# A fused attention and feed-forward kernel: four loads for the first group, two helpers moved, and a new order of calls

## What is computed

```python
x = x + attn_ref(layernorm(x), ...)   # linear attention, then a feed-forward of 1024 with gelu
x = x + ffn_ref(layernorm(x), ...)    # ternary weights, gelu, layernorm over 1024
```

## Time and profile before

| | |
|---|---|
| median of 3 runs | 464.06 us (463.73 to 464.63) |
| the profiled execution | 462.83 us |
| its span on the core, first to last instruction | 461.1 us |
| mean granted TensorE clock | 0.993 |
| PE (TensorE matmul) busy | 441.1 us, 96% |
| DVE (VectorE) busy | 369.7 us, 80% |
| ACT (ScalarE) busy | 321.1 us, 70% |
| POOL (GpSimd) busy | 185.7 us, 40% |
| chain that ended last | PE 84%, DVE 6%, issue 4%, POOL 2%, ACT 2%, DMA 1% |

### The profile page before, as it was taken

How to read it: one execution, slowest core, us unless ns; L and a number is a source line. 1 busy time by engine, 2 the same in 40 slices (tenths; PEclk the granted TensorE clock), 3 DMA queues, 4 the chain that set the end, 5 groups by cost and what they waited for, 6 DMA issues and landing times.

```text
span 461.1 us, 8907 instructions
## 1 busy us (share of the span) xinstructions
PE 441.1 (96%) x2980; PEld 399.3 (87%) x2980; DVE 369.7 (80%) x1212; ACT 321.1 (70%) x603; POOL 185.7 (40%) x188
## 2 busy tenths in 40 slices
...
GB/s 245 110 92 137 1 2 1 1 23 2 8 61 2 25 0 70 1 24 1 2 69 2 23 1 71 0 25 1 0 70 1 24 1 24 1 1 23 7 19 47
DMA packets 10045, 14.09 MB, mean 31 GB/s; under 512 B 784, under 2 KB 9104, under 8 KB 9488
## 3 DMA queue, kind: packets, MB, share of 16 engines
...
...
## 4 chain that ended last, share of the span: by engine, by line
PE 84%; DVE 6%; issue 4%; POOL 2%; ACT 2%; DMA 1%; DVEq 0%; POOLq 0%; ACTq 0%
PE bank_f L410 13%; PE bank_p L440 12%; PE bank_y L201 6%; PE bank_y L202 6%; PE bank_y L203 6%; PE bank_f L201 6%; PE bank_f L203 6%; PE bank_y L424 6%; PE bank_f L202 6%; PE bank_a L201 4%; PE bank_a L203 4%; PE bank_a L202 4%; PE bank_a L209 3%; PE bank_f L209 2%; PE bank_a L308 1%
## 5 line engine op out<-in xcount | busy, mean ns | idle before, releaser
L1146 POOL TENSOR_TENSOR rs<-ve,neg_half 128x2 f32<-128x2 f32 x48 | 33.7, 702 | 208.6 <-DVE ve L835 207.2
L896 DVE TENSOR_TENSOR h_lo<-bank_f,h_hi 128x512 fp32r<-128x512 f32 x60 | 41.3, 688 | 34.7 <-ACT h_hi L649 34.6
L201 PE MATMUL bank_y<-wf_hi,h_hi 128*128 128x256 f32 x240 | 67.1, 280 | 0.0
L202 PE MATMUL bank_y<-wf_lo,h_hi 128*128 128x256 f32 x240 | 67.0, 279 | 0.0
L203 PE MATMUL bank_y<-wf_hi,h_lo 128*128 128x256 f32 x240 | 67.0, 279 | 0.0
L440 PE MATMUL bank_p<-wpj_t,g_hi 128*128 128x256 f32 x256 | 64.3, 288 | 0.6 <-DVE y_yc L1040 0.6
L1031 DVE SCALAR_TENSOR_TENSOR g_lo<-bank_y,vec,g_hi 128x256 fp32r<-128x256 f32 x128 | 55.7, 477 | 9.3 <-ACT g_hi L678 8.2
L440 PE MATMUL bank_p<-wpj_t,g_lo 128*128 128x256 f32 x256 | 62.3, 279 | 0.0
L678 ACT ACTIVATE g_hi<-bank_y,vec 128x256 fp32r<-128x256 f32 x128 | 53.1, 481 | 10.3 <-PE bank_y L424 8.1
L641 ACT ACTIVATE bank_f<-bank_f,f_bias 128x512 f32<-128x512 f32 x64 | 42.4, 664 | 23.8 <-PE bank_f L203 23.4
L410 PE MATMUL bank_f<-wfc_t,z3T_hi 128*128 128x512 f32 x128 | 53.6, 419 | 0.5 <-DVE z3T_lo L896 0.5
...
## 6 DMA issues: line engine op xcount, KB each, us to landing
...
h<-in_f SPq DMA_DIRECT2D x1, 1024.0 KB, 7.6
y_yc<-in_f SPq DMA_DIRECT2D x1, 1024.0 KB, 10.0
h<-in_fc SPq DMA_DIRECT2D x1, 1024.0 KB, 4.8
h<-in_pj SPq DMA_DIRECT2D x1, 1024.0 KB, 4.7
...
```

The source lines that it names most:

```text
L201: pe.matmul(ps, w[0], r[0], start=start, stop=False, skip_group_check=skip)
L202: pe.matmul(ps, w[0], r[1], start=False, stop=False, skip_group_check=skip)
L896: dve.tensor_tensor(dst, b, hi.bitcast(F32), ALU.subtract).then_inc(s[ready], 1)
L1146: pool.tensor_tensor(rs[n][:, 2 * h:2 * h + 2], ve[n][:, 2 * h:2 * h + 2], neg_half[:, 0:2], ALU.pow).then_inc(s[f"ln{n + 1}_rs"], 1)
```

## The change

1. `load_x(0)` issues four loads, one tile of 128 tokens each, in place of two. The even tiles signal `x_first0` and `x_first1`, the odd tiles the old semaphores. VectorE takes the statistics of the even tiles in a new `ln1_st0`, and `ln1_stats(0, h)` makes only those of the odd tile and then goes on as before.
2. `wide_cols` goes from VectorE to GpSimd, which multiplies a constant block `inv_d` (a new memset in `consts`) with a broadcast column.
3. All lists of calls are ordered anew, with the same calls in them: in `first` above all, and in `step` and `last`.

```diff
+        inv_d = sb("inv_d", [P, P])
...
                 for h in range(2):
-                    sp.dma_start(x_two[g % 2][:, 2 * h:2 * h + 2, :], tiles(x, g, h)).then_inc(s[x_loaded(g, h)], 16)
+                    if g == 0:
+                        t = 2 * h
+                        sp.dma_start(x_two[0][:, t, :], x[0][t * P:(t + 1) * P, :]).then_inc(s[f"x_first{h}"], 16)
+                        sp.dma_start(x_two[0][:, t + 1, :], x[0][(t + 1) * P:(t + 2) * P, :]).then_inc(s[x_loaded(0, h)], 16)
+                    else:
+                        sp.dma_start(x_two[g % 2][:, 2 * h:2 * h + 2, :], tiles(x, g, h)).then_inc(s[x_loaded(g, h)], 16)
...
+            def ln1_st0(g, h):
+                dve.wait_ge(s[f"x_first{h}"], 16)
+                dve.bn_stats(bn[0][:, 2 * h, :], x_two[0][:, 2 * h, :]).then_inc(s["ln1_bn"], 1)
...
                 for t in (2 * h, 2 * h + 1):
+                    if g == 0 and t % 2 == 0:
+                        continue
...
+                pool.memset(inv_d[:], 1.0 / D).then_inc(s["inv_set"], 1)
...
-                for n, col in enumerate((vb_c[:, 0:1], vb_c[:, 1:2], less_w[:, 0:1], less_w[:, 1:2])):
-                    dve.tensor_scalar(wide[:, n, :], mean_w[:], float(H) / D, col, ALU.mult, ALU.mult).then_inc(s["wide_ready"], 1)
...
+                for n, col in enumerate((vb_c[:, 0:1], vb_c[:, 1:2], less_w[:, 0:1], less_w[:, 1:2])):
+                    pool.tensor_tensor(wide[:, n, :], inv_d[:], col.to_broadcast([P, P]), ALU.mult).then_inc(s["wide_ready"], 1)
...
+                    if g == 0:
+                        pool.wait_ge(s[f"x_first{h}"], 16)
```

The new lists, as far as the prediction speaks of them. TensorE, `first` and the first half of `step`:

```diff
                 qkb(); tu(0, 0); tu(0, 1); wvo_mm(); qk_mm(0); bvo(); scores(0); v_mm(0, 0); v_mm(0, 1)
+                attend(0, 0); attend(0, 1); attend(0, 2); tu(1, 0); attend(0, 3); f1b(); tz2(0, 0); tz2(0, 1)
+                theta_sum(0); tu(1, 1); f1(0, 0); qk_mm(1); f1(0, 1); f1(0, 2); theta_sum(1); f2(0, 0); f1(0, 3)
...
                 f1(0, 7); f2(0, 5); f2(0, 6); f2(0, 7); v_mm(1, 0); v_mm(1, 1); attend(1, 0); attend(1, 1)
+                tz3(0, 0); attend(1, 2); fc(0, 0, 0); tz3(0, 1); attend(1, 3); fc(0, 0, 1); fc(0, 1, 0); fc(0, 1, 1)
...
+                f1(g, 4); f1(g, 5); f2(g, 0); f2(g, 1); f2(g, 2); f1(g, 6); f2(g, 3); scores(g + 1); f2(g, 4)
```

ScalarE, `first` and a part of `step`:

```diff
+                tables(); u_norm(0, 0); u_norm(0, 1); wqk_hi(); u_hi(0, 0); u_hi(0, 1); wf1_hi(0); wvo_copy()
+                wf1_hi(1); wf1_hi(2); qk_exp(0); wf1_hi(3); qk_hi(0); k_dup(0); wvo_hi(); n1(0); ae_hi(0); af_hi(0)
+                v_hi(0, 0); ad_hi(0); v_hi(0, 1); u_norm(1, 0); wf2_hi(0); wf2_hi(1); wf2_hi(2); wf2_hi(3)
+                u_hi(1, 0); u_norm(1, 1); abs_part(0); z2_norm(0, 0); abs_part(1); z2_norm(0, 1); z2_hi(0, 0)
+                z2_hi(0, 1); u_hi(1, 1); abs_part(2); gelu(0, 0); h_hi(0, 0); abs_part(3); gelu(0, 1); ln3_hi()
...
+                g_hi(g - 1, 1, 3); qk_exp(g + 1); gelu(g, 4); h_hi(g, 4); gelu(g, 5); qk_hi(g + 1); k_dup(g + 1)
```

VectorE and GpSimd, `first`:

```diff
+                consts(); ln1_st0(0, 0); ln1_stats(0, 0); ln1_st0(0, 1); ln1_stats(0, 1); dcol(); ln1_shift(0, 0)
+                u_odd(0, 0); ln1_shift(0, 1); n1_ve(0); u_odd(0, 1); wqk_lo(); u_lo(0, 0); u_lo(0, 1); qk_bias_add()
+                n1_shift(0); ln1_stats(1, 0); qk_max(0); qk_sum(0); selectors(); wvo_add(); qk_lo(0); wvo_lo()
+                ln1_stats(1, 1); ae_mask(0); af_mask(0); ad_mask(0); ln1_shift(1, 0); ae_lo(0); af_lo(0); v_lo(0, 0)
+                ad_lo(0); v_lo(0, 1); attn_out(0, 0); ln2_stats(0, 0); attn_out(0, 1); attn_out(0, 2)
...
+                consts(); ln1_rstd(0, 0); ln1_rstd(0, 1); wide_cols(); n1_rstd(0); wf1_lo(0); wf1_lo(1)
+                ln1_rstd(1, 0); wf1_lo(2); n1o(0); wf1_lo(3); ln1_rstd(1, 1); wf2_lo(0); ln2_rstd(0, 0)
```

More of the change, by code:

```diff
@@ L460, in step @@
[L460 to L463, removed]
-                tz3(g, 0); attend(g + 1, 2); tz3(g, 1); attend(g + 1, 3); fc(g, 0, 0); fc(g, 0, 1); fc(g, 1, 0)
@@ L1043, in first @@
             def first():
-                consts(); ln1_stats(0, 0); ln1_stats(0, 1); dcol(); ln1_shift(0, 0); u_odd(0, 0); ln1_shift(0, 1)
-                n1_ve(0); u_odd(0, 1); u_lo(0, 0); wide_cols(); wqk_lo(); n1_shift(0); u_lo(0, 1); qk_bias_add()
-                ln1_stats(1, 0); qk_max(0); qk_sum(0); wvo_add(); selectors(); ln1_shift(1, 0); qk_lo(0); wvo_lo()
-                ln1_stats(1, 1); af_mask(0); ad_mask(0); ae_mask(0); af_lo(0); ad_lo(0); v_lo(0, 0); ae_lo(0)
-                v_lo(0, 1); attn_out(0, 0); ln2_stats(0, 0); attn_out(0, 1); ln1_shift(1, 1); attn_out(0, 2)
@@ new lines, in first @@
+                ln2_stats(0, 3); ln2_var(0, 1); n1_ve(1); z2_odd(0, 0); ln2_shift(0, 1); z2_odd(0, 1); u_lo(1, 0)
+                z2_lo(0, 0); z2_lo(0, 1); threshold(0); f1_bias_add(); u_lo(1, 1); ternary(0); h_lo(0, 0)
+                ternary(1); h_lo(0, 1); threshold(1); qk_max(1); ln3_lo(); h_lo(0, 2); ternary(2); h_lo(0, 3)
+                ternary(3); qk_sum(1); h_lo(0, 4); n1_shift(1); qk_lo(1); h_lo(0, 5); ad_mask(1); ln1_stats(2, 0)
+                h_lo(0, 6); ln1_stats(2, 1); ae_mask(1); af_mask(1); h_lo(0, 7); ad_lo(1); ae_lo(1); af_lo(1)
@@ new lines, in first @@
+                n1_shift(2); z2_lo(1, 1); ln4_shift(0, 0)
+            def step(g):
+                g_lo(g - 1, 0, 3); g_lo(g - 1, 1, 0); h_lo(g, 0); h_lo(g, 1); u_lo(g + 1, 0); u_lo(g + 1, 1)
+                g_lo(g - 1, 1, 1); output(g - 1, 0); h_lo(g, 2); qk_max(g + 1); g_lo(g - 1, 1, 2); h_lo(g, 3)
+                g_lo(g - 1, 1, 3); ln4_stats(g - 1, 2); qk_sum(g + 1); h_lo(g, 4); ln4_stats(g - 1, 3); qk_lo(g + 1)
+                ln4_var(g - 1, 1); h_lo(g, 5); ae_mask(g + 1); af_mask(g + 1); ln4_shift(g - 1, 1); ad_mask(g + 1)
+                ad_lo(g + 1); h_lo(g, 6); af_lo(g + 1); h_lo(g, 7); ae_lo(g + 1); y_sum(g, 0); ln3_stats(g, 0)
+                y_sum(g, 1); v_lo(g + 1, 0); ln3_stats(g, 1); ln3_shift(g, 0); v_lo(g + 1, 1); ln3_shift(g, 1)
@@ L1078, in last @@
+                z2_lo(g + 1, 0); ln4_stats(g, 0); g_lo(g, 0, 2); n1_ve(g + 2); z2_lo(g + 1, 1); ln1_shift(g + 2, 0)
+                ln4_stats(g, 1); ln4_var(g, 0); ln1_shift(g + 2, 1); n1_shift(g + 2); ln4_shift(g, 0)
             def last():
[L1080 to L1082 removed]
```

191 lines of the change are left out of this document (85 added, 106 removed).

## The result

| | kernel before | changed kernel |
|---|---|---|
| median | 464.06 us (463.35 to 464.63) | 466.22 us (465.45 to 467.00) |
| ratio, 95% interval | | 1.0053 [1.0038, 1.0069] |
| measured once more beside other runs | 463.46 us | 466.01 us, 1.0053 [1.0035, 1.0071] |
| the profiled execution, its span | 462.83, 461.1 | 466.78, 465.1 |
| mean granted clock in it | 0.993 | 0.980 |

The change makes the kernel slower, by 2.2 to 2.6 us. The forecast was 464.1, its range ended at 465.9: wrong, and to the slow side.

What follows compares the result with a forecast made beforehand. TensorE was taken as full from 76.2 to 432.2 us, so only start and end could gain. Start +0.28, stretch 43.6 to 76 -0.25, steps and tail 0 summed to +0.03: 464.1 us, range 462.9 to 465.9.

Steps and rivals of the forecast that it cites:

- x_odd's landing: Start, loads behind x: x_odd lands 0.7 us later, bounds 0 and 0.95, so qk_max(0) moves from 13.98 to 14.68.
- vec: Start: the vec load, behind two more issues, lands at 6.6 us instead of 5.8, making everything up to wvo_mm 0.5 to 0.6 later.
- The gap before qk_mm(0), attend(0,0), tu(1,0), wide_cols: Start: PE waits of 0.43 and 0.63 close, tu(1,0) before f1b adds 0.44, wide_cols takes 0.35 each on GpSimd.
- ln1_shift out of the way: Start, DVE: ln1_shift(1,0) no longer stands ahead of qk_lo(0), -0.32 us.
- scores(0) to f1b: Start, PE: attend(0,2) goes earlier, -0.36 us, and tu(1,0) placed before f1b adds +0.44.
- f1b and pj: End of the start: f1b ends +0.46 us later, pj lands at 39.35, so abs_part(2) and f1(0,2) come +0.28 later.
- The repeated steps: Repeated steps: same PE work, k_lo placed near 215.7 ahead of scores(g+1) due at 216.14, so 0.
- the tail: Tail: f2h's last product decides when ln3(7) starts, as late as before: 0, with 0.3 either way.
- Rival (b): Repeated steps: scores(g+1) waits for k_lo, 0.3 us in five steps and last, 1.8 in all, 465.9; chance 0.18.
- tz3 into the gap: 43.6 to 76 us: tz3(0,0) fills PE's wait for v_lo(1,1), -0.44, with fc(0,0,1) +0.19, together -0.25 us.
- rival (a): Start: the loads behind x are not delayed, sum -0.67 us, 463.4, or 463.1 with the tail's gain; chance 0.28.

Runs made afterwards that it cites:

- e12: The changed kernel itself, unaltered, run and profiled once more: 466.01 us, ratio 1.0053.
- e9: Kernel before with new step and last lists, but transposes again between fc products and y_cpj(7) again behind ln4_rstd(7,0): 464.24 us, 1.0007.
- e8: Kernel before with the new lists of step and last alone: 465.00 us, 1.0024.
- e1: Changed kernel with x(0) in two loads again, the rest kept: 464.37 us, 1.0014.
- e5: Changed kernel with x(0) in two loads and the old lists of step and last: 464.34 us, 1.0014.
- e3: Changed kernel with the old lists of step and last, four loads kept: 464.84 us, 1.0017.
- e2: Kernel before with the four loads of x(0) and the separate ln1_st0 alone: 464.68 us, 1.0017.
- e14: Changed kernel with two loads, ln1_stats(1,0) behind qk_sum(0), some f1 readers on ACT later, transposes and y_cpj(7) put back in step and last: 464.75 us, 1.0014.
- e16: Same as e14 but with x(0) in four loads: 464.76 us, 1.0015.
- e6: Changed kernel with wide_cols back on VectorE, inv_d and its memset removed: 466.05 us, 1.0053.
- e4: Changed kernel with ln1_stats(1,0) behind qk_sum(0) on DVE and all wf1_hi behind k_dup(0) on ACT: 466.59 us, 1.0058.
- e10: Changed kernel with x(0) in two loads, transposes between fc products and y_cpj(7) behind ln4_rstd(7,0) again: 464.09 us, 1.0010.

## Why the prediction was wrong

**x_odd's landing (+0.70, "bounds 0 and 0.95").** The step that failed most. The place was right: ln1_stats(1,0) on DVE ahead of qk_max(0), with a longer DMA wait. The size was 2.13, and the bound was wrong. It rested on the same bytes being asked for only 0.95 later; but from 7 to 10 us the DMA engines were 51 to 74% busy in place of 99 to 102%, and between like kernels the landing varied more than the issues moved. With two loads x_odd landed at 12.7 to 13.8 (seven kernels), with four and rows in its place at 13.1 to 14.9 (eight). The means are 13.1 and 14.2, so four loads are worth about 1.1 on average and 2 in the changed kernel.

**vec ("I take 6.6").** Wrong, and in direction: it landed at 5.4, earlier than before (5.8), so the start gained 0.47 on less_w. The two more issues ahead of it (3.14 in place of 2.30) did not hold it up: it took 2.3 us to land in place of 3.5.

**The gap before qk_mm(0), attend(0,0), tu(1,0), wide_cols.** Right. qk_mm(0) started at 10.66 without a wait. No wait stood before attend(0,0). tu(1,0) took its place before f1b. wide_cols took 0.38 to 0.44 each (I took 0.35) and was hidden:

```profile
6.48 0.76 POOL L1125 TENSOR_TENSOR xa<-inv_d,vec 128x128 f32<-128x128 f32 x2
7.20 0.88 POOL L1125 TENSOR_TENSOR xa<-inv_d,less_w 128x128 f32<-128x128 f32 x2
```

**ln1_shift out of the way (-0.32).** More than that: from qk_max(0) to scores(0) it took 5.56 in place of 6.32, so -0.76.

**scores(0) to f1b (-0.36+0.44=+0.08).** +1.03 in the first profile and +0.15 in the second of the same kernel (10.38), so the order was sized rightly. The sum had no term for the granted clock, which was 0.50 in that stretch of the first profile.

**f1b and pj (+0.46, +0.28).** f1b came 2.24 later and f1(0,2) 2.88 later. pj, issued at 36.43, landed 4.8 later at 41.2, just as ACT came to abs_part(2) at 41.27; before it PE's tu(1,1) had held ACT for 0.58. In e12 abs_part(2) did wait for pj, 0.44 us. But the chain that the prediction followed, pj to abs_part(2) to f1(0,2), isn't the one that ended last in either profile: f1(0,2) waited for h_lo(0,0), which started at 45.73 (44.92 in e12), although h_hi(0,0), which it needs, was ready on ACT at 45.03 (44.53). DVE came to it late from the passes of ternary(0), 1.95 us longer beside GpSimd's xpb(0) and xs(0). "ACT and DVE get there by 38.6 as I place them" had no term for that, though the earlier trace rows shows the same kind of slowing.

**The repeated steps (0) and the tail (0).** Both wrong, 0.55 and 0.5 us. "Their PE work is the same" holds for the work and not for its order. Putting the transposes between products again took the step from 52.90 to 52.82 (e9). And the tail's look at waits left out what runs beside what: z3_odd(7,1) took 0.98 us beside GpSimd in place of 0.41. Rival (b) had the sign and the time (465.9), but not the mechanism: no step waits for k_lo.

**tz3 into the gap (-0.25).** Right in kind: tz3(0,0) ran at 74.82, between attend(1,1) and attend(1,2), and PE's idle time from 43.6 to 76.2 fell from 1.2 to 0.6. But the end did not come nearer by as much: from f1(0,2) to fc(1,0,0) it took 85.49 us in place of 85.44, with the 0.11 of one step in it, so about 0.06 of the 0.25 is left.

**The range.** Its lower end, 462.9, isn't what its own parts give (463.1). A slower kernel had a chance of 0.24, but by a wait on k_lo that no step has.

**How it adds up.** The ratio 1.0053 is 2.5 us. In the profiles the parts are x_odd's way (+1.97-0.76), scores(0) to f1b with its clock (+1.03 and +0.15 in two profiles), the passes beside GpSimd (up to +0.65), the steps (+0.55) and the tail (+0.5). In the medians they don't add. Steps and tail cost 0.9 to 1.1 with the old start (e8), nothing in the new start with two loads (e1 and e5) and 1.4 to 1.7 with four (e3 and the changed kernel). The four loads cost 0.6 to 0.8 in the old order (e2), 0.1 to 0.5 beside the old steps (e3 and e5), 1.8 beside the new ones, and nothing with x_odd and f1 off the way (e14 and e16). So each part is shown to cost by itself or in its stretch, and the size of the whole is not explained. The new start with two loads and old steps (e5) is at +0.65, against the -0.67 of rival (a); the passes and the seam can make up 1.2 of that difference. Open is also why the changed kernel, e6, e12 and e16 have x_odd at 14.7 to 14.9, and e2 and e4, with the same nine issues ahead, at 13.1 to 13.3. Some of it is no property of the kernels: where loads and lists of the start are the same, single profiles have x_odd up to 1.0 us apart (e1, e5 and e10: 12.8, 13.0, 13.8; the changed kernel, e12 and e3: 14.8, 14.8, 14.1).
